# Two-layer attention and FFN kernel: the maximum chunks of the second layer in pairs on the two row halves of the array, and the query product in double parts

## The chip, the cores and the metric

The kernel runs on one core of a Trainium2 chip. The metric is device time in microseconds (us) from one launch to its end; the median of three runs is taken. The profile is one further execution of the same program.

## The reference, cut to what matters

Two layers run over a sequence of 8 batches of 100 tokens of 256 features; each has a cross attention and a feed-forward part. The change lies in the cross attention of the second layer (16 heads, 1444 keys for each batch, 64 latent dimensions):

```python
q_hk  = (hidden_q @ Wq.T).reshape(Bv, Sv, H, K)
q_big = rope(einsum('bshk,hkq->bshq', q_hk, w_kc_q))       # 192 wide
kv_r  = rope(kv_c)                                         # 64 wide
q_r   = einsum('bshq,hqr->bhsr', q_big, W_qr)
k_r   = einsum('bld,hdr->bhlr', kv_r, W_kr)
scores = einsum('bhsr,bhlr->bhsl', q_r, k_r)
attn   = softmax(scores, axis=-1)
ctx_c  = einsum('bhsl,bld->bhsd', attn, kv_r)
...
```

The kernel multiplies the weights of the query side together beforehand, so that a query meets the 64 roped key values directly. The softmax subtracts a maximum for each query, and any value near the largest score serves, since it cancels in the quotient.

## The kernel before

The second layer is worked in 16 **periods** u, two for each batch b; a period holds 8 heads of 100 queries, 800 columns. It has 24 **slots** (`LANE`), numbered `at` = 0 to 23, or s = 0 to 47 through a batch. In each slot k the function `scores(k)` puts one block of 120 keys by 400 queries in bank 0 or 1 of PSUM, as two matmuls (line 1167): a first one of 128 rows, in which the high parts of the queries meet the high and low parts of the keys (called *hi* below), and a second of 65 rows for the low parts of the queries and the maximum (*lo*). ACT takes the exponential of the block (line 1631). `scores(k)` waits until ACT has done block k - 2. After every eighth slot, `values` sums four double blocks into the context on the two column halves of the array (line 1179). POOL adds the weights up, off to the side.

While period u runs, three things are made ready for later ones, each laid into the slots by hand:

- **The maximum of period u + 1.** Seven blocks of 128 queries (the last has 32) times three stretches of 482 keys make 21 chunks (`MC`). A chunk c is one matmul of 128 rows (line 1147, `max_chunk`), into banks 3 and 4 in turn, and one reduction on DVE (line 1931, `reduce_max`). It stands in slot `at` = 1 + c. A chunk waits for the reduction of the chunk two before it. After the last, in slot 21, `join_max` takes the maximum of the three columns (line 1938); in slot 23 `turn_max` on PE waits for it and transposes it (line 1153). ACT copies that out, and a DMA lays it down as the row that the scores of u + 1 use.
- **The query product of period u + 2**, `q_big`, in six parts in the slots `at` = 1 to 6 and 9 to 14 (lines 1091 and 1096, four matmul instructions a part), then `rope` on DVE after slots 7 and 15, and `q_latent` after slot 23 (line 1118).
- **The FFN of batches before**: attention output in slots s = 17 to 20 (line 1202), gate and up product, and on DVE `residual` in slot s = 21 (lines 1956 to 1960), `quantise_x` in s = 23, `quantise_h` in s = 13, 17, 20 and 23.

Every engine works off its own queue in program order and waits on semaphores. An instruction that waits holds back all that stands behind it on its engine. The chunks of period 0 have no slots to lie in: they run in a stretch ahead of the loop, with `q_big` and `rope` of period 1 among them.

## Time and profile before

| | |
|---|---|
| median of three runs | 955.08 us (953.51 to 961.84) |
| profiled execution | 955.46 us, of which the span of the trace is 953.7 |
| PE (TensorE matmul) busy | 847.4 us, 89% of the span |
| DVE (VectorE) busy | 582.8 us, 61% |
| POOL busy | 448.9 us, 47% |
| ACT (ScalarE) busy | 415.9 us, 44% |
| mean granted clock of TensorE | 0.93 |

The loop over the 16 periods runs from 321.7 us to about 926 us. A period takes between 29 and 42 us. Matmuls are pipelined: the time of one in the trace runs from its start to its modelled end, so what a matmul costs the engine is read from the start of one to the start of the next. The line numbers in the tables are those of the kernel before.

### The profile page before, as it was taken

The numbers are of one execution on the slowest core, as the hardware profiler recorded it, in microseconds if no ns is written. First come the engines' busy times: TensorE is split into PE (matmuls) and PEld (weight loads), VectorE is DVE, ScalarE is ACT, GpSimd is POOL, SyncE is SP. The second block draws the span as 40 slices with busy tenths as digits, with TensorE's granted clock in tenths as the row PEclk, the third lists the DMA queues.
The fourth block names the chain that finished last, engine by engine and source line by source line (L and its number), as shares of the span: only waits on it lengthen the run. The fifth ranks groups of instructions, "written<-read, shape, count | busy, mean of one in ns | idle before, by whom it ended". The sixth has DMA issues, their size and how long they took to land.

```text
span 953.7 us, 15582 instructions
## 1 busy us (share of the span) xinstructions
PE 847.4 (89%) x5844; PEld 629.2 (66%) x5844; DVE 582.8 (61%) x1112; ACT 415.9 (44%) x896; POOL 448.9 (47%) x465
## 2 busy tenths in 40 slices
PE   4998879989987799998989889899898988989884
PEld 3666756888965567766767667676676766766442
DVE  3537854222275567577587588668658748757445
ACT  2357851212121354544534544554454463454531
POOL 3000006500050187767657576666675755557530
PEclk8879989989997799999989999999999999999976
DMA  9560026589310000000000000010000000000000
GB/s 194 184 198 2 2 64 241 208 303 344 109 36 17 16 2 11 20 7 10 17 9 10 21 10 2 10 30 1 10 22 10 10 5 10 2 14 10 8 6 9
DMA packets 42167, 52.28 MB, mean 55 GB/s; under 512 B 12230, under 2 KB 35704, under 8 KB 41836
## 3 DMA queue, kind: packets, MB, share of 16 engines
q1 hardware_dynamic: 41068, 49.63, 16.6%
q0 software_dynamic: 1024, 1.64, 0.6%
q8 instruction: 47, 0.77, 0.3%
q14 instruction: 28, 0.23, 0.1%
HBM read 45.80 MB, written 5.36 MB: 54 GB/s over the span
## 4 chain that ended last, share of the span: by engine, by line
PE 68%; DVE 16%; ACT 7%; issue 4%; DMA 3%; POOL 1%; POOLq 0%; SPq 0%; DVEq 0%; ACTq 0%
PE ps L1167 13%; PE ps L1179 10%; PE ps L1147 7%; PE ps L1091 5%; PE ps L1015 5%; PE ps L1202 3%; PE ps L1118 3%; PE ps L969 3%; PE ps L1028 3%; PE ps L1096 2%; DVE nm L1931 2%; ACT sm L1424 2%; DMA xs<-xs_scratch 2%; DVE xyz L1902 1%; DVE h L1992 1%
## 5 line engine op out<-in xcount | busy, mean ns | idle before, releaser
L592 POOL TENSOR_TENSOR acc<-acc,pt 120x800 f32<-120x800 f32 (+1 forms) x157 | 301.6, 1921 | 123.5 <-ACT pt L1631 91.3
L1631 ACT ACTIVATE pt<-ps 120x400 f32<-120x400 f32 (+1 forms) x384 | 189.4, 504 | 237.1 <-PE ps L1167 229.4
L1931 DVE TENSOR_REDUCE nm<-ps 128x1 f32<-128x482 f32 (+1 forms) x336 | 215.7, 655 | 109.0 <-PE ps L1147 105.7
L1167 PE MATMUL ps<-qh,khl 128*120 128x400 f32 (+1 forms) x384 | 167.9, 437 | 24.0 <-ACT pt L1631 23.6
L1147 PE MATMUL ps<-khl,qh 128*128 128x482 f32 (+1 forms) x336 | 136.1, 408 | 10.6 <-DVE nm L1931 9.1
L1179 PE MATMUL ps<-pt,kv 120*64 120x400 f32 (+1 forms) x768 | 145.0, 514 | 0.0
L1167 PE MATMUL ps<-ql,kh 65*120 65x400 f32 (+1 forms) x384 | 137.2, 357 | 0.0
L1167 PEld LDWEIGHTS ps<-qh,khl 128*120 128x120 f32 (+1 forms) x384 | 72.9, 190 | 70.6 <-ACT pt L1631 34.3
L1179 PEld LDWEIGHTS ps<-pt,kv 120*64 120x64 f32 (+1 forms) x768 | 52.8, 140 | 66.6 <-issue 58.3
L614 POOL TENSOR_TENSOR rstd<-veps,mhalf 100x1 f32<-100x1 f32 (+2 forms) x19 | 13.0, 682 | 167.5 <-DVE veps L1765 115.4
L1091 PEld LDWEIGHTS ps<-x3T,wqb 128*128 128x128 f32 x512 | 76.6, 195 | 6.7 <-DVE xyz L1902 1.7
L1091 PE MATMUL ps<-x3T,wqb 128*128 128x100 f32 x512 | 75.0, 274 | 2.7 <-ACT x3T L1388 1.4
L1167 PEld LDWEIGHTS ps<-ql,kh 65*120 65x120 f32 (+1 forms) x384 | 73.6, 192 | 4.4
L1147 PEld LDWEIGHTS ps<-khl,qh 128*128 128x128 f32 (+1 forms) x336 | 61.6, 184 | 22.3 <-DVE nm L1931 18.9
L592 POOL TENSOR_TENSOR acc<-pt,pt 121x800 f32<-121x800 f32 x16 | 30.5, 1907 | 93.3 <-ACT pt L1631 93.3
L1015 PE MATMUL ps<-xsT,egu 128*128 128x128 f32 x448 | 53.5, 278 | 1.0 <-DVE hs L1857 0.6
L1015 PEld LDWEIGHTS ps<-xsT,egu 128*128 128x128 f32 x448 | 52.9, 195 | 1.8 <-ACT xsT L1388 1.3
L1202 PE MATMUL ps<-bmat,ct 128*100 128x256 f32 x128 | 38.3, 428 | 13.8 <-DVE ct L1952 13.1
L1912 DVE TENSOR_TENSOR ql<-ps,qh 64x400 fp32r<-64x400 f32 x32 | 18.2, 570 | 49.8 <-ACT qh L1551 49.6
L667 POOL DMA_INDIRECT xn<-ys_scratch,slot x8 | 8.6, 1078 | 81.9 <-DMA ys_scratch<-ysb 79.9
L1902 DVE TENSOR_TENSOR xyz<-ps,ropeq 64x200 f32<-64x200 f32 x128 | 46.2, 361 | 1.3
L1551 ACT ACTIVATE qh<-ps 64x400 fp32r<-64x400 f32 x64 | 31.9, 498 | 31.9 <-PE ps L1118 31.4
(273 smaller groups left out, 1270.5 us busy)
## 6 DMA issues: line engine op xcount, KB each, us to landing
egu<-_L_ffn_gate_up_proj_dram SPq DMA_DIRECT2D x14, 1024.0 KB, 6.0
edn<-in_L_ffn_down_proj_dram SPq DMA_DIRECT2D x14, 512.0 KB, 6.8
spread<-inv_scratch SPq DMA_DIRECT2D x30, 100.0 KB, 2.7
craw<-in_ctx_dram SPq DMA_DIRECT2D x8, 360.0 KB
wo_n<-in_L_xattn_Wo_dram SPq DMA_DIRECT2D x1, 2048.0 KB, 11.3
wq_n<-in_L_xattn_Wq_dram SPq DMA_DIRECT2D x1, 2048.0 KB, 8.0
xs_scratch<-zero SPq DMA_DIRECT2D x1, 1792.0 KB, 9.8
xs<-xs_scratch SPq DMA_DIRECT2D x14, 128.0 KB, 5.9
```

Of the source, the lines that this page charges most:

```text
L592: nc.gpsimd.tensor_tensor(total[r, :, :], before[r, :, :], pt[j % PT_BUF][r, :, :], ALU.add).then_inc(p_added, 1)
L969: last = mm(ps[:, 2 * (k % 2) + a, 0:HT], sgu[:, c, a, 128 * m:128 * m + 128], xnT[:, c, HT * n:HT * n + HT], start=c == 0, stop=c == DC - 1)
L1015: last = mm(ps[:, 2 * (t % 2) + a, TR * m:TR * m + TR], egu[t % EBUF][:, c, FI * a + 128 * m:FI * a + 128 * m + 128], xsT[t % 2][:, c, :], ...
L1091: mm(ps[:, 6, S * part:S * part + S], wqb[:, c, h, 0:128], x3T[:, c, :], start=c == 0, stop=c == DC - 1)
L1147: mm(ps[0:w, 3 + m % 2, 0:MN], qh[u % 2][:, 128 * i:128 * i + w], khl[b % 2][:, MSTART[n]:MSTART[n] + MN], start=True, stop=True).then_inc ...
L1167: last = mm(ps[0:key_rows(t), k % 2, 0:HT], lhs[:, keys], rhs[:, HT * a:HT * a + HT], start=first, stop=not first)
L1179: last = mm(ps[CD * a:CD * a + CD, 2, 0:HT], kv[b % KV_BUF][r, t, :], pt[j % PT_BUF][r, a, :], start=t == 0, stop=t == KT - 1)
L1202: last = mm(ps[0:S, 6, 0:D], ct[:, S * i:S * i + S], bmat[:, i, :], start=i == 0, stop=i == GH - 1)
L1551: last = nc.scalar.activation(qh[u % 2][p:p + CD, HT * a:HT * a + HT], ps[CD * a:CD * a + CD, 5, 0:HT], ACT.Copy)
L1631: nc.scalar.activation(pt[j % PT_BUF][0:rows, k % 2, :], ps[0:rows, k % 2, 0:HT], ACT.Exp).then_inc(p_ready, 1)
L1902: last = tt(o[CD * j:CD * j + CD, 2, e:HG:2, :], ps[CD * e:CD * e + CD, 7, 0:HT // 2].rearrange("p (i q) -> p i q", i=HG // 2), ropeq[CD * ...
L1931: nc.vector.tensor_reduce(nm3[0:w, i, n:n + 1], ps[0:w, 3 + m % 2, 0:MN], AX.X, ALU.max).then_inc(m_reduced, 1)
```

## The change

`max_chunk` becomes `max_pair`. Eleven pairs (`MP`) take the place of 21 chunks, and stand in every second slot, `at` = 2, 4 to 22 (`MAX_AT`). A matmul of a pair has 64 rows instead of 128. The even chunk takes rows 0 to 63 of the array with the high parts of the keys (`kh1`), the odd chunk rows 64 to 127, where `khl` also holds high parts. So the low parts of the keys no longer enter the maximum. The even chunk writes bank 3, the odd one bank 4; the eleventh pair has one chunk only. A pair waits for the reduction of the pair just before it. DVE reads both banks in one instruction of two stretches of 482.

`q_big` stands in slots 1, 3, 5 and 9, 11, 13, two parts at a time.

```diff
--- before.py
+++ after.py
@@ -74,7 +74,9 @@
 GU = 2 * HT
 MT = -(-GU // 128)
 MC = 3 * MT
-MAX_FROM, TURN_MAX_AT = 1, 23
+MP = -(-MC // 2)
+MAX_AT, TURN_MAX_AT = (2, 4, 6, 8, 10, 12, 14, 16, 18, 20, 22), 23
+QB_AT = (1, 3, 5)
 X3_BANK = (4, 7, 5)
 KEEP_AT, INVERT_AT, DIVIDE_AT = 1, 9, 15
 
@@ -1131,21 +1133,23 @@
                                 ident[0:key_rows(t), 0:key_rows(t)])
                 last.then_inc(k_turned, 1)
 
-            def max_chunk(u, c):
-
-                b, p, m = u // PAIRS, u % PAIRS, MC * u + c
-                if c == 0:
+            def max_pair(u, i):
+
+                b, p = u // PAIRS, u % PAIRS
+                if i == 0:
                     pe.wait_ge(q_hi, u + 1)
                     if p == 0:
                         pe.wait_ge(k_kept, 3 * (b + 1))
                     if u:
                         pe.wait_ge(m_kept, u)
-                if m >= 2:
-                    pe.wait_ge(m_reduced, m - 1)
-                i, n = c // 3, c % 3
-                w = m_rows(i)
-                mm(ps[0:w, 3 + m % 2, 0:MN], qh[u % 2][:, 128 * i:128 * i + w], khl[b % 2][:, MSTART[n]:MSTART[n] + MN],
-                   start=True, stop=True).then_inc(m_done, 1)
+                if MP * u + i:
+                    pe.wait_ge(m_reduced, MP * u + i)
+                for c in range(2 * i, min(2 * i + 2, MC)):
+                    q, n, r = c // 3, c % 3, slice(CD * (c % 2), CD * (c % 2) + CD)
+                    w = m_rows(q)
+                    keys = khl if c % 2 else kh1
+                    mm(ps[0:w, 3 + c % 2, 0:MN], qh[u % 2][r, 128 * q:128 * q + w], keys[b % 2][r, MSTART[n]:MSTART[n] + MN],
+                       start=True, stop=True).then_inc(m_done, 1)
 
             def turn_max(u):
 
@@ -1280,9 +1284,9 @@
                 q_big(1, 0, part)
             pe.wait_ge(tails_set, 2)
             pe.wait_ge(fq_kept, 6)
-            for c in range(MC):
-                max_chunk(0, c)
-                if c == MC // 2:
+            for i in range(MP):
+                max_pair(0, i)
+                if i == MP // 2:
                     for part in range(6):
                         q_big(1, 1, part)
             turn_x3(1)
@@ -1293,10 +1297,11 @@
                     k, u, at = SLOTS * b + s, PAIRS * b + s // LANE, s % LANE
                     f, x = at // PHASE, at % PHASE
                     scores(k)
-                    if u + 1 < NU and MAX_FROM <= at < MAX_FROM + MC:
-                        max_chunk(u + 1, at - MAX_FROM)
-                    if u + 2 < NU and f < 2 and 1 <= x <= 6:
-                        q_big(u + 2, f, x - 1)
+                    if u + 1 < NU and at in MAX_AT:
+                        max_pair(u + 1, MAX_AT.index(at))
+                    if u + 2 < NU and f < 2 and x in QB_AT:
+                        for part in range(2):
+                            q_big(u + 2, f, 2 * QB_AT.index(x) + part)
                     if b + 1 < B and s in KEY_SLOT:
                         turn_keys(b + 1, KEY_SLOT.index(s))
                     if b + 2 < B and s == X_SLOT:
@@ -1921,18 +1926,19 @@
                 tt(khl[b % 2][0:CD, k0:k0 + n], ps[0:CD, 5, 0:n], kh1[b % 2][0:CD, k0:k0 + n].bitcast(F32), ALU.subtract)\
                     .then_inc(k_kept, 1)
 
-            def reduce_max(u, c):
-
-                if c == 0 and u:
+            def reduce_max(u, i):
+
+                if i == 0 and u:
                     dve.wait_ge(max_ready, u)
-                m, i, n = MC * u + c, c // 3, c % 3
-                w = m_rows(i)
-                dve.wait_ge(m_done, m + 1)
-                nc.vector.tensor_reduce(nm3[0:w, i, n:n + 1], ps[0:w, 3 + m % 2, 0:MN], AX.X, ALU.max).then_inc(m_reduced, 1)
+                n = min(2, MC - 2 * i)
+                w = m_rows(2 * i // 3)
+                dve.wait_ge(m_done, MC * u + 2 * i + n)
+                nc.vector.tensor_reduce(nm3[:, :, :].rearrange("p i n -> p (i n)")[0:w, 2 * i:2 * i + n], ps[0:w, 3:3 + n, 0:MN],
+                                        AX.X, ALU.max).then_inc(m_reduced, 1)
 
             def join_max(u):
 
-                dve.wait_ge(m_reduced, MC * (u + 1))
+                dve.wait_ge(m_reduced, MP * (u + 1))
                 if u >= 2:
                     dve.wait_ge(m_turned, u - 1)
                 nc.vector.tensor_reduce(nmx[u % 2][:, :], nm3[:, :, :], AX.X, ALU.max, negate=True).then_inc(max_ready, 1)
@@ -2025,13 +2031,13 @@
             low_keys(0, 2)
             low_q(0)
             dve.wait_ge(tails_set, 2)
-            for c in range(MC):
-                if c == 1:
+            for i in range(MP):
+                if i == 1:
                     rope(1, 0)
-                reduce_max(0, c)
-                if c == MC // 2:
+                reduce_max(0, i)
+                if i == MP // 2:
                     norm_x3(1)
-                if c == MC // 2 + 2:
+                if i == MP // 2 + 1:
                     rope(1, 1)
             join_max(0)
             low_q(1)
@@ -2041,9 +2047,9 @@
                     f, x = at // PHASE, at % PHASE
                     if u and u + 1 < NU and at == 0:
                         low_q(u + 1)
-                    if u + 1 < NU and MAX_FROM <= at < MAX_FROM + MC:
-                        reduce_max(u + 1, at - MAX_FROM)
-                        if at == MAX_FROM + MC - 1:
+                    if u + 1 < NU and at in MAX_AT:
+                        reduce_max(u + 1, MAX_AT.index(at))
+                        if at == MAX_AT[-1]:
                             join_max(u + 1)
                     if b >= 2 and s == HN_SLOT:
                         hidden_norm(b - 2)
```

On PE, at the start of the period u = 3 (slots 0 to 2). Before:

```order
L1167 MATMUL ps<-qh_192,khl_188 121x400
L1167 MATMUL ps<-ql_194,kh_190 121x400
L1167 MATMUL ps<-qh_192,khl_188 121x400
L1167 MATMUL ps<-ql_194,kh_190 121x400
L1147 MATMUL ps<-khl_187,qh_191 128x482
L1091 MATMUL ps<-x3T,wqb 128x100 x2
L1167 MATMUL ps<-qh_192,khl_188 121x400
L1167 MATMUL ps<-ql_194,kh_190 121x400
L1147 MATMUL ps<-khl_187,qh_191 128x482
L1091 MATMUL ps<-x3T,wqb 128x100 x2
```

After:

```order
L1171 MATMUL ps<-qh_192,khl_188 121x400
L1171 MATMUL ps<-ql_194,kh_190 121x400
L1171 MATMUL ps<-qh_192,khl_188 121x400
L1171 MATMUL ps<-ql_194,kh_190 121x400
L1093 MATMUL ps<-x3T,wqb 128x100 x4
L1171 MATMUL ps<-qh_192,khl_188 121x400
L1171 MATMUL ps<-ql_194,kh_190 121x400
L1151 MATMUL ps<-kh_189,qh_191 128x482
L1151 MATMUL ps<-khl_187,qh_191 128x482
```

Slot 1 has lost its chunk and holds two parts of the query product; slot 2 holds both chunks of the first pair, one behind the other.

On PE, the end of the period u = 4, slots 21 to 23 and the transpose of the maximum. Before:

```order
L1167 MATMUL ps<-qh_191,khl_187 120x400
L1167 MATMUL ps<-ql_193,kh_189 120x400
L1147 MATMUL ps<-khl_187,qh_192 32x482
L1167 MATMUL ps<-qh_191,khl_187 120x400
L1167 MATMUL ps<-ql_193,kh_189 120x400
L1167 MATMUL ps<-qh_191,khl_187 120x400
L1167 MATMUL ps<-ql_193,kh_189 120x400
L1153 MATMUL ps<-ident,nmx_207 7x128
```

After:

```order
L1171 MATMUL ps<-qh_191,khl_187 120x400
L1171 MATMUL ps<-ql_193,kh_189 120x400
L1171 MATMUL ps<-qh_191,khl_187 120x400
L1171 MATMUL ps<-ql_193,kh_189 120x400
L1151 MATMUL ps<-kh_189,qh_192 32x482
L1171 MATMUL ps<-qh_191,khl_187 120x400
L1171 MATMUL ps<-ql_193,kh_189 120x400
L1157 MATMUL ps<-ident,nmx_207 7x128
```

The last chunk of the maximum has moved one slot nearer to the transpose that needs its result.

On DVE, the same place, from `quantise_h` of slot 20 on. Before:

```order
L1931 TENSOR_REDUCE nm_205<-ps 32x1 x2
L2000 TENSOR_SCALAR h_214<-h_214,qsc 100x1024
L1931 TENSOR_REDUCE nm_205<-ps 32x1
L1938 TENSOR_REDUCE nmx_207<-nm_205 128x7
L1956 TENSOR_TENSOR x_sb<-x_sb,ps 100x256
L1958 BN_STATS stats_80<-x_sb 100x6
L1959 BN_AGGR mv_81<-stats_80 100x2
L1960 TENSOR_SCALAR veps_82<-mv_81 100x1
L1966 TENSOR_SCALAR xn_210<-x_sb,mv_81 100x256
```

After:

```order
L1936 TENSOR_REDUCE nm_205<-ps 32x2
L2006 TENSOR_SCALAR h_214<-h_214,qsc 100x1024
L1962 TENSOR_TENSOR x_sb<-x_sb,ps 100x256
L1964 BN_STATS stats_80<-x_sb 100x6
L1965 BN_AGGR mv_81<-stats_80 100x2
L1966 TENSOR_SCALAR veps_82<-mv_81 100x1
L1936 TENSOR_REDUCE nm_205<-ps 32x1
L1944 TENSOR_REDUCE nmx_207<-nm_205 128x7
L1972 TENSOR_SCALAR xn_210<-x_sb,mv_81 100x256
```

The four operations of `residual` stood behind the joined maximum and now stand ahead of its last reduction.

## Rows read from the trace of the kernel before

Some names: in the tables a line such as L1147 is a chunk's matmul, L1167 a score matmul (`qh,khl` is *hi*, `ql,kh` is *lo*), L1091 a part of `q_big`, L1179 `values`, L1118 `q_latent`, L1153 `turn_max`.

**Rows 1.** Page, part 4: the chain that ended last, shares by engine.

```profile
PE 68%; DVE 16%; ACT 7%; issue 4%; DMA 3%; POOL 1%; POOLq 0%; SPq 0%; DVEq 0%; ACTq 0%
```

**Rows 2.** Groups by form, DVE, 500 to 700 us: count | busy, mean ns | idle before.

```profile
L1931 DVE TENSOR_REDUCE nm<-ps 128x1 f32<-128x482 f32 x90 | 58.2, 658 | 28.0 <-PE ps L1147 27.3
...
L1994 DVE TENSOR_REDUCE qsc<-h 100x1 f32<-100x1024 f32 x2 | 2.4, 1208 | 0.0
```

**Rows 3.** Timeline of PE, slots with chunks alone: start, us, engine, line, op.

```profile
610.66 0.38 PE L1147 MATMUL ps<-khl,qh 128*128 128x482 f32 x1
610.88 0.34 PE L1167 MATMUL ps<-qh,khl 128*120 128x400 f32 x1
611.06 0.35 PE L1167 MATMUL ps<-ql,kh 65*120 65x400 f32 x1
611.25 0.38 PE L1147 MATMUL ps<-khl,qh 128*32 128x482 f32 x1
614.63 0.66 PE L1167 MATMUL ps<-qh,khl 128*120 128x400 f32 x1 [3.01 <-ACT pt L1631]
```

**Rows 4.** Timeline of PE, one slot with a q_big part.

```profile
600.84 0.42 PE L1167 MATMUL ps<-qh,khl 128*120 128x400 f32 x1
601.10 0.35 PE L1167 MATMUL ps<-ql,kh 65*120 65x400 f32 x1
...
601.88 0.42 PE L1167 MATMUL ps<-qh,khl 128*120 128x400 f32 x1
```

**Rows 5.** Timeline of PE around a block of values (128x64 halves).

```profile
604.61 0.34 PE L1073 MATMUL ps<-ident,xn 100*128 100x100 f32 x2
604.88 2.91 PE L1179 MATMUL ps<-pt,kv 120*64 120x400 f32 x16
607.71 0.45 PE L1167 MATMUL ps<-qh,khl 128*120 128x400 f32 x1
608.00 0.35 PE L1167 MATMUL ps<-ql,kh 65*120 65x400 f32 x1
```

**Rows 6.** Timeline of PE, 32-row groups of the array, layer 1.

```profile
62.51 0.96 PE L773 MATMUL ps<-kT,qT 32*100 32x100 f32 x32 [0.57 <-issue]
```

**Rows 7.** Timeline of PE, last period: slots without chunks.

```profile
912.68 0.44 PE L1167 MATMUL ps<-qh,khl 128*120 128x400 f32 x1
...
913.90 0.44 PE L1167 MATMUL ps<-qh,khl 128*120 128x400 f32 x1 [0.23 <-ACT pt L1631]
```

**Rows 8.** Timeline of PE, end of a period (u = 4).

```profile
496.36 0.38 PE L1147 MATMUL ps<-khl,qh 128*32 128x482 f32 x1
...
499.21 0.28 PE L1153 MATMUL ps<-ident,nmx 128*7 128x128 f32 x1
```

**Rows 9.** Timeline of DVE, the same stretch.

```profile
496.77 0.65 DVE L1931 TENSOR_REDUCE nm<-ps 32x1 f32<-32x482 f32 x1 [0.85 <-PE ps L1147]
497.35 0.73 DVE L2000 TENSOR_SCALAR h<-h,qsc 100x1024 f32<-100x1024 f32 x1
498.30 0.65 DVE L1931 TENSOR_REDUCE nm<-ps 32x1 f32<-32x482 f32 x1 [0.22 <-PE ps L1147]
498.98 0.17 DVE L1938 TENSOR_REDUCE nmx<-nm 128x7 f32<-128x21 f32 x1
499.07 0.41 DVE L1956 TENSOR_TENSOR x_sb<-x_sb,ps 100x256 f32<-100x256 f32 x1
...
500.28 0.35 DVE L1966 TENSOR_SCALAR xn<-x_sb,mv 100x256 f32<-100x256 f32 x1
```

**Rows 10.** Waits of PE, 320 to 900 us: in total, times, longest.

```profile
PE ps L1167 <- ACT pt L1631: 20.2, 10, 3.0
PE ps L1202 <- DVE ct L1952: 13.1, 6, 2.8
```

**Rows 11.** Timeline of DVE, the maxima ahead of the loop.

```profile
293.14 0.66 DVE L1931 TENSOR_REDUCE nm<-ps 128x1 f32<-128x482 f32 x1
...
317.38 0.18 DVE L1938 TENSOR_REDUCE nmx<-nm 128x7 f32<-128x21 f32 x1
```


## The prediction

> **What bounds the kernel now.** I read the page's chain of waits first: 68% of the chain that ended last is PE, 16% DVE [rows 1]. So PE's own time counts nearly everywhere in the loop, and DVE's where PE waits for it. The second view is PE's timeline, from which I take the start of one matmul to the start of the next. In a slot that holds scores and a chunk, *hi* takes 0.18, *lo* 0.19 and the chunk 0.22: 0.59 us [rows 3]. A slot with a part of `q_big` on top takes 1.04, and *hi* to *lo* is there 0.26 instead of 0.18, since *hi* follows another kind of matmul [rows 4]; that leaves 0.38 for the part. Third, the floor under a slot: in the last period two slots of bare scores take 1.22 [rows 7]. PE waits there for ACT, two banks being all that scores have, so emptying slots below 0.61 each gains nothing. Fourth, the waits of PE: 20.2 us on ACT and 13.1 on the divided context [rows 10]; the wait on the maximum's reductions is too short to stand among them. DVE takes 0.658 us for a chunk [rows 2], against slots of 0.59 to 1.04: it keeps up, just.
>
> **The change, part by part.**
>
> *The matmuls of a pair.* Does the array run both halves at once? The trace before has no 64-row pair of this type. Two near cases overlap. `values`, on two column halves, gets through 16 instructions of 400 columns in 2.83 [rows 5], 0.044 for each 100 columns, against 0.38 / 4 = 0.095 for an instruction of `q_big` of the same type with 100 columns on the whole array [rows 3, 4]. In layer 1, 32 instructions on four 32-row groups take 0.96 [rows 6], under 0.03 each. So I take the two streams of a pair as one: 0.22 instead of 0.44.
>
> *The change of mode around a pair.* Scores use the whole array, a pair halves; each pair is one way in and one way back. Price, from the block of `values`: two transposes start at 604.61 and should last 0.18, `values` starts at 604.88, 0.09 late. Its 16 instructions of 400 columns should need, at 0.0417 for 100 columns (two cycles of 2.4 GHz a column, which the 0.095 of `q_big` is near to, and two halves at once), 2.67; scores start after 2.83, 0.16 late; and *hi* to *lo* is 0.29 instead of 0.18, another 0.11 [rows 5]. Together 0.36. I take 0.33 for a pair, which has no second pass to line up. Bounds: 0.15 (a row half that loads while the array drains) and 0.40. A pair is then 0.22 + 0.33 = 0.55 against 0.44, 0.11 more; ten full pairs in a period make +1.1.
>
> The Trainium skill, TensorEngine Tiling (Array Packing), Theoretical Speedup, gives up to 2x for a contraction of 64, which would favour this change; the same page says under Key Properties that changing the mode drains the engine, with no price. By the first alone a pair would save 0.22, by the second with the trace's price it loses 0.11. The rows of `values` show both, the overlap and the drain, so the sum goes with them.
>
> *`q_big` in double parts.* The same instructions, in 6 slots instead of 12. Six fewer returns to *hi*, each 0.26 - 0.18 = 0.08 [rows 3, 4]: -0.5 a period. `rope` still starts after slot 7, its inputs being ready earlier (slot 5); no gain behind it, since the reductions ahead of it on DVE are the same work.
>
> Together +0.6 in each of the 14 periods with `q_big` (u = 0 to 13): 8.4. In six of them PE waits for the divided context in slot 17 [rows 10], which comes from DVE, and hides what PE lost in slots 13 to 16, about 0.25 each: -1.5. **Term A: +7** (-18 to +18 over the bounds).
>
> *DVE's reductions.* One instruction of 964 values instead of two of 482. From 0.658 for 482 and 1.208 for 1024 [rows 2] a value costs 1.01 ns, so 1.15 against 1.32. It saves 1.7 a period of an engine that is 61% busy. Where DVE is late (slots 12 to 17 of even periods) the count of values between is the same, so PE's wait in slot 17 stays. Taken at nothing.
>
> *One pair in flight.* Before, chunk m waited for chunk m - 2. Now a pair waits for the pair just before. The circle is: pair to reduction 0.49 (a chunk's went from 496.36 to 496.77 [rows 8, 9], and the second matmul of a pair starts later by up to 0.08), reduction 1.15, back to PE 0.08 (an estimate, such as lies between the join at 498.98 + 0.17 and `turn_max` at 499.21): 1.72. With `q_big` two slots take about 2.1 and cover it; so does attention output in slots 17 to 20. It shows where slots are thin: two slots of 0.55 + 4 x 0.18 = 1.3. That is u = 14 (five intervals), u = 1 (three) and u = 0 (one or two), each 0.45 longer. **Term B: +4** (1 to 9; the high end if low keys and `quantise_h` on DVE push reductions past the next pair).
>
> *The end of a period, `turn_max`.* This is the large term. `turn_max` on PE stands ahead of `q_latent` and `values`, and waits for the joined maximum. Before, the last chunk lay in slot 21; now it lies in slot 22, and on DVE `residual` of slot 21 has come ahead of it. For u = 4: the chunk of slot 20 started at 496.36 and `turn_max` at 499.21 [rows 8]. With the change, on DVE: reduction of the pair of slot 20 from 496.85 (the chunk's was at 496.77) to 498.00; `quantise_h` until 498.95 (it takes 0.95 to the next start); `residual` 1.21 (499.07 to 500.28), until 500.16; last reduction 0.65, 500.81; join 0.2; `turn_max` at 501.07 [rows 9]. That is 1.86 later. PE itself would be there at about 499.4, so this is a wait of 1.7, and nothing later gives it back: what follows on PE (`q_latent`, `values`, next scores) moves with it. It meets the six periods u = 4, 6 to 14: 11.2. In u = 2, without `quantise_h`, 1.86 - 0.95, about 1. In u = 0 and the seven odd periods there is no `residual`; from the last chunk to `turn_max` 0.49 + 0.65 + 0.2 + 0.06 = 1.4 must pass, and PE fills 0.55 + 0.45 with its work; 0.4 is left, partly there before (0.2 in u = 4), and part of these stretches runs at the low clock, where PE is the slower: 0.3 each, 2.4. **Term C: +15** (7 to 20).
>
> *Ahead of the loop.* The 21 chunks of period 0 run at DVE's pace from 293.14 to 317.38 [rows 11]. 21 reductions of 0.658 are 13.8, two ropes and a norm the rest, with a wait for `q_big`. Now ten times 1.15 and 0.65, 12.2, saves 1.6, but seven or eight pairs with nothing of DVE's between them expose 0.57 each, 4.3. **Term D: +2.6** (0 to 5).
>
> Low keys, `quantise_x` and `turn_xq` keep their places; ACT, POOL and the DMAs have no instruction moved. I take all of that at nothing; it is covered by PE's 2.1 us between pairs, and without that cover a low-key step of 0.6 would come on top once.
>
> **Sum:** 7 + 4 + 15 + 2.6 = 28.6 on the profiled 955.46, which is 0.4 above the median of 955.08: 983.7. Forecast **983 us**, 2.9% slower.
>
> **The rivals.**
>
> *The halves pay (faster).* If the change of mode costs a row pair 0.02 instead of 0.33, a pair is 0.24, saves 0.20, and A is 14 x (-2.0 - 0.5) = -35. With B, C and D: -13, 942. Break-even of the whole is a price of 0.13: A then is 14 x (10 x (0.35 - 0.44) - 0.5) = -20. For it: the layer 1 groups overlap well [rows 6]. Against: 0.36 for a block of `values` [rows 5]. By the page's 2x alone it would come out here. Chance 0.12.
>
> *No wait at `turn_max`.* If DVE is earlier there, or slot 22 and 23 are held by ACT anyway (two bare slots need 1.22 [rows 7]), C falls to 1 or 2: 970. Against: the order of DVE's queue leaves no way around `residual`. Chance 0.14.
>
> *The clock falls.* After a wait of 3.01 the next *hi* took 0.66 instead of 0.42 [rows 3, 4], so the granted clock had gone to the lower level. If the 1.7 us waits of six periods do that too, for as long as the waits on ACT did, some 1.7 more each: +10, 993. Chance 0.17.
>
> *The two 64-row matmuls run one after the other.* A pair is 0.44 + 0.33, 0.33 more, A is 14 x (3.3 - 0.5) = 39: 1016. No row shows this type of matmul on row halves, all others overlap. Chance 0.07.
>
> The forecast itself: 0.50.
>
> **The numbers.** About 1% (9.6 us) is what this kernel's runs can tell from no change. Faster by over 1%: the first rival and a little of A's low end, 0.15. Within 1%: A near its low end with a small C, 0.14. Slower: 0.71. For 8 in 10 I leave out the sequential case and most of the fast one: 955 to 1001, which takes in A at a price of 0.15 (965) and the clock rival with its own spread.
>
> **What the profile after would show.** Right: both matmuls of a pair start within some 0.05 of each other; *lo* to the next *hi* around a pair is near 0.75 to 0.8 in all; PE waits 1.5 to 2 for the joined maximum before `turn_max` in even periods from u = 4; reductions take 1.15; the stretch ahead of the loop ends some 2.5 later. Wrong: a pair costing PE under 0.4; no wait before `turn_max`; the slots 17 to 20 of even periods shorter than before; or a stall that I have not placed, since DVE has one pair of slack less in every slot.

## The result

The changed kernel takes 1021.12 us (median of 4, 1013.51 to 1023.43) against 954.3 for the kernel before: 7.1% slower, ratio 1.0709, 95% interval 1.0654 to 1.0765. The forecast was 983 with a range up to 1001. The direction was right, and less than half of the size. Medians and ratios here leave out runs that lie more than 1.5% above the fastest of their kernel, which meets two of the six runs of e2 and one of the four of e4.

In the kernel after, the lines stand a little lower: L1171 is the score matmuls, L1151 a matmul of a pair, L1093 and L1098 the query product, L1206 attention output, L1120 `q_latent`, L1183 `values`, L1157 `turn_max`; on DVE L1936 is the reduction and L1944 the join. In the runs below the numbers shift again by a few lines.

The page of the profile after, parts 1, 4 and 5 (busy time; chain; count | busy, mean ns | idle before). The span is 1021.5 us, 67.8 more than before.

```profile
PE 895.8 (88%) x5844; PEld 603.8 (59%) x5844; DVE 561.9 (55%) x952; ACT 415.9 (41%) x896; POOL 448.8 (44%) x465
...
PE 69%; DVE 14%; ACT 7%; issue 5%; DMA 4%; POOL 1%; SPq 0%; POOLq 0%; ACTq 0%; DVEq 0%
...
L1936 DVE TENSOR_REDUCE nm<-ps 128x2 f32<-128x964 f32 (+2 forms) x176 | 195.7, 1112 | 190.5 <-PE ps L1151 190.0
...
L1151 PE MATMUL ps<-kh,qh 64*128 64x482 f32 (+1 forms) x176 | 89.0, 506 | 18.3 <-DVE nm L1936 18.3
```

DVE does what was forecast: a reduction of two banks takes 1.112 us on the mean over all forms, 21 us less busy time in all. PE is still 69% of the chain [rows 1]. A matmul of a pair stands at 506 ns, against some 400 for a chunk before.

PE's timeline after, slots 1 to 3 of the period u = 7 (start, us, engine, line):

```profile
618.72 1.03 PE L1093 MATMUL ps<-x3T,wqb 128*128 128x100 f32 x8
619.53 0.42 PE L1171 MATMUL ps<-qh,khl 128*121 128x400 f32 x1
619.79 0.35 PE L1171 MATMUL ps<-ql,kh 65*121 65x400 f32 x1
620.07 0.48 PE L1151 MATMUL ps<-kh,qh 64*128 64x482 f32 x1
620.08 0.48 PE L1151 MATMUL ps<-khl,qh 64*128 64x482 f32 x1
620.49 0.44 PE L1171 MATMUL ps<-qh,khl 128*121 128x400 f32 x1
620.77 0.35 PE L1171 MATMUL ps<-ql,kh 65*121 65x400 f32 x1
620.96 1.03 PE L1093 MATMUL ps<-x3T,wqb 128*128 128x100 f32 x8
```

The two matmuls of a pair start 0.01 us apart: the halves do overlap. But from *lo* to the pair is 0.28, from the pair to the next *hi* 0.42, and *hi* to *lo* 0.28; before it was 0.19, 0.22 and 0.18 [rows 3]. That is 0.62 above a pair of slots without chunks, where two chunks cost 0.44. And the eight instructions of a double query part take 0.81 (620.96 to about 621.77), two single parts 0.76.

The end of the even period u = 6. First PE, then DVE:

```profile
610.46 0.40 PE L1151 MATMUL ps<-kh,qh 64*32 64x482 f32 x1
...
611.07 0.35 PE L1171 MATMUL ps<-ql,kh 65*120 65x400 f32 x1
612.78 0.28 PE L1157 MATMUL ps<-ident,nmx 128*7 128x128 f32 x1 [1.36 <-DVE nmx L1944]
```

```profile
608.83 1.15 DVE L1936 TENSOR_REDUCE nm<-ps 32x2 f32<-32x964 f32 x1 [3.10 <-PE ps L1151]
609.91 0.73 DVE L2006 TENSOR_SCALAR h<-h,qsc 100x1024 f32<-100x1024 f32 x1
610.67 0.42 DVE L1962 TENSOR_TENSOR x_sb<-x_sb,ps 100x256 f32<-100x256 f32 x1
...
611.88 0.64 DVE L1936 TENSOR_REDUCE nm<-ps 32x1 f32<-32x482 f32 x1
612.55 0.17 DVE L1944 TENSOR_REDUCE nmx<-nm 128x7 f32<-128x21 f32 x1
```

This is the order of [rows 8, 9] with `residual` (L1962) ahead of the last reduction (L1936), and it cost about what was worked out: from the reduction of the pair of slot 20 to `turn_max` 612.78 - 608.83 = 3.95, where the prediction had 501.07 - 496.85 = 4.22. PE idles 1.36 in front of it, where the prediction had 1.7. The same wait stands in front of `turn_max` in each of the six periods forecast, the even ones from u = 4 to 14, at 1.34 to 1.36.

The waits of PE from 340 to 960 us (total, times, longest), and the circle of one pair in the thin slots of u = 14 (L1151 on PE):

```profile
PE ps L1157 <- DVE nmx L1944: 9.1, 8, 1.4
PE ps L1151 <- DVE nm L1936: 3.3, 7, 1.1
```

```profile
936.05 0.48 PE L1151 MATMUL ps<-kh,qh 64*128 64x482 f32 x1 [0.37 <-DVE nm L1936]
...
937.82 0.48 PE L1151 MATMUL ps<-kh,qh 64*128 64x482 f32 x1 [0.36 <-DVE nm L1936]
```

1.77 from pair to pair, against 1.72 in the prediction. The whole period u = 14, before and then after (the columns of this view are the stretch, its length, then busy time and count of PE, PEld, DVE, ACT and POOL, the granted clock, DMA share and GB/s):

```profile
858.86:888.32 29.46, 28.46 (x141) 17.64 (x139) 22.46 (x44) 13.83 (x29) 20.42 (x12) 1.00 0.03 8
...
920.82:956.74 35.92, 32.59 (x140) 16.82 (x138) 22.45 (x34) 13.54 (x29) 22.13 (x13) 0.90 0.03 6
```

It grew by 6.5 us, and part of it now lies at the lower clock. Where TensorE runs at the lower clock (granted 0.50 from 300 to 324 us), the circle is longer. Here is DVE ahead of the loop:

```profile
296.11 1.16 DVE L1936 TENSOR_REDUCE nm<-ps 128x2 f32<-128x964 f32 x1 [0.16 <-PE ps L1151]
...
303.89 1.16 DVE L1936 TENSOR_REDUCE nm<-ps 128x2 f32<-128x964 f32 x1 [0.89 <-PE ps L1151]
305.94 1.16 DVE L1936 TENSOR_REDUCE nm<-ps 128x2 f32<-128x964 f32 x1 [0.89 <-PE ps L1151]
...
324.10 0.17 DVE L1944 TENSOR_REDUCE nmx<-nm 128x7 f32<-128x21 f32 x1
```

Between 303.89 and 305.94 it is 2.05. The stretch from first reduction to join takes 28.0, against 24.2 before [rows 11]. It also begins 3.0 later (296.11 against 293.14), with no edit of the change ahead of it: over the traces of all runs here that first reduction starts anywhere from 287.3 to 299.5 us. Two single executions can differ by that much before the second layer begins.

Last, one stretch at the end of an odd period (u = 7): slot 19, where PE waits 3 us for ACT, up to the start of the next period (the same view as for u = 14). Before:

```profile
611.47:623.86 12.39, 9.35 (x78) 6.29 (x77) 4.31 (x8) 7.50 (x14) 7.97 (x8) 0.86 0.12 38
```

After (it begins a little earlier, in slot 18):

```profile
645.60:661.60 16.00, 12.56 (x81) 7.62 (x79) 4.76 (x7) 7.71 (x14) 8.03 (x8) 0.68 0.11 30
```

The mean granted clock is 0.86 before and 0.68 after. With the two levels at 1 and 0.5 (2.4 and 1.2 GHz), that is 12.39 x 0.14 x 2 = 3.5 us at the lower one before, and 16.0 x 0.32 x 2 = 10.2 after. The same 3 us wait is followed by three times as long a low stretch. Over the fifteen periods u = 0 to 14 the mean granted clock is 0.97 before (321.68 to 888.32) and 0.92 after (328.13 to 956.74), some 34 and 99 us at the lower level. Of the 65 more, 37 lie in the odd periods and 20 in u = 0 and u = 14, the periods with thin slots, which had none before.

### The profile page after: what moved, and what is told of

Its sections match the earlier page's. It is cut to its first block, busy times and chain, and to the rows that moved or that the text cites. A ratio compares the mean times of both kernels' runs of the same rounds, so it can differ in the third digit from the quotient of the medians.

```text
span 1021.5 us, 15422 instructions
## 1 busy us (share of the span) xinstructions
PE 895.8 (88%) x5844; PEld 603.8 (59%) x5844; DVE 561.9 (55%) x952; ACT 415.9 (41%) x896; POOL 448.8 (44%) x465
## 4 chain that ended last, share of the span: by engine, by line
PE 69%; DVE 14%; ACT 7%; issue 5%; DMA 4%; POOL 1%; SPq 0%; POOLq 0%; ACTq 0%; DVEq 0%
PE ps L1171 14%; PE ps L1183 11%; PE ps L1151 7%; PE ps L1093 6%; PE ps L1120 5%; DVE nm L1936 4%; PE ps L1017 3%; PE ps L1206 3%; PE ps L1098 2%; PE ps L971 2%; DMA xs<-xs_scratch 2%; ACT sm L1429 2%; PE ps L1030 2%; DVE xyz L1907 1%; DVE h L1998 1%
## 5 line engine op out<-in xcount | busy, mean ns | idle before, releaser
L1936 DVE TENSOR_REDUCE nm<-ps 128x2 f32<-128x964 f32 (+2 forms) x176 | 195.7, 1112 | 190.5 <-PE ps L1151 190.0
L1171 PE MATMUL ps<-qh,khl 128*120 128x400 f32 (+1 forms) x384 | 179.3, 467 | 25.4 <-ACT pt L1636 25.0
L1183 PE MATMUL ps<-pt,kv 120*64 120x400 f32 (+1 forms) x768 | 146.1, 517 | 0.0
L1171 PE MATMUL ps<-ql,kh 65*120 65x400 f32 (+1 forms) x384 | 141.3, 368 | 0.0
L1171 PEld LDWEIGHTS ps<-qh,khl 128*120 128x120 f32 (+1 forms) x384 | 74.5, 194 | 95.2 <-issue 55.8
L1151 PE MATMUL ps<-kh,qh 64*128 64x482 f32 (+1 forms) x176 | 89.0, 506 | 18.3 <-DVE nm L1936 18.3
L1183 PEld LDWEIGHTS ps<-pt,kv 120*64 120x64 f32 (+1 forms) x768 | 53.3, 141 | 67.0 <-issue 64.5
L1151 PE MATMUL ps<-khl,qh 64*128 64x482 f32 (+1 forms) x160 | 80.9, 506 | 0.0
L1171 PEld LDWEIGHTS ps<-ql,kh 65*120 65x120 f32 (+1 forms) x384 | 76.4, 199 | 2.7
L1151 PEld LDWEIGHTS ps<-kh,qh 64*128 64x128 f32 (+1 forms) x176 | 31.3, 178 | 71.8 <-issue 44.5
L1093 PE MATMUL ps<-x3T,wqb 128*128 128x100 f32 x512 | 67.9, 278 | 2.7 <-ACT x3T L1393 1.4
L1093 PEld LDWEIGHTS ps<-x3T,wqb 128*128 128x128 f32 x512 | 67.8, 196 | 3.7 <-ACT x3T L1393 1.6
L1206 PE MATMUL ps<-bmat,ct 128*100 128x256 f32 x128 | 41.7, 457 | 14.5 <-DVE ct L1958 13.9
L1120 PE MATMUL ps<-xyz,amat 128*64 128x100 f32 x768 | 49.1, 301 | 4.3 <-DVE h L1988 2.2
```

Of the source, the lines that this page charges most:

```text
L1093: mm(ps[:, 6, S * part:S * part + S], wqb[:, c, h, 0:128], x3T[:, c, :], start=c == 0, stop=c == DC - 1)
L1120: last = mm(ps[CD * a:CD * a + CD, 5, S * i:S * i + S], amat[:, 2 * HG * p + HG * a + i, j, :], xyz[a][:, j, i, :], start=j == 0, stop=j == 2)
L1151: mm(ps[0:w, 3 + c % 2, 0:MN], qh[u % 2][r, 128 * q:128 * q + w], keys[b % 2][r, MSTART[n]:MSTART[n] + MN], start=True, stop=True).then_in ...
L1171: last = mm(ps[0:key_rows(t), k % 2, 0:HT], lhs[:, keys], rhs[:, HT * a:HT * a + HT], start=first, stop=not first)
L1183: last = mm(ps[CD * a:CD * a + CD, 2, 0:HT], kv[b % KV_BUF][r, t, :], pt[j % PT_BUF][r, a, :], start=t == 0, stop=t == KT - 1)
L1206: last = mm(ps[0:S, 6, 0:D], ct[:, S * i:S * i + S], bmat[:, i, :], start=i == 0, stop=i == GH - 1)
```

## The experiments

Each was timed beside runs of the kernel before on the same chip; ratios are to those. The expectations name three theories. Theory 1 is the matmuls' own cost, above all the change of mode for the halves; theory 2 is the late slots and the single pair in flight; theory 3 is the low clock.

**e3: double query parts alone**, in the kernel before.

```diff
-                    if u + 2 < NU and f < 2 and 1 <= x <= 6:
-                        q_big(u + 2, f, x - 1)
+                    if u + 2 < NU and f < 2 and x in (1, 3, 5):
+                        for part in range(2):
+                            q_big(u + 2, f, x - 1 + part)
```

> The kernel before with the double query parts alone (slots 1, 3, 5 and 9, 11, 13), chunks as before. My prediction had this as a gain of 0.5 a period, 7 us: 947. The trace of the changed kernel shows eight instructions of a double part 0.11 apart, four of a single part 0.09 apart: if a part alone hides its weight loads behind the long matmuls around it, this costs 0.15 to 0.2 x 84: 12 to 17 us more than before, 967 to 971.

951.08 against 951.08, ratio 0.9963 (0.9919 to 1.0006): nothing. Neither the gain of my prediction nor the loss expected here. PE's timeline of two slots:

```profile
599.64 0.35 PE L1167 MATMUL ps<-ql,kh 65*120 65x400 f32 x1
599.82 0.38 PE L1147 MATMUL ps<-khl,qh 128*128 128x482 f32 x1
600.04 1.03 PE L1096 MATMUL ps<-x3T,wqt 128*128 128x100 f32 x8
600.85 0.43 PE L1167 MATMUL ps<-qh,khl 128*120 128x400 f32 x1
```

The double part takes 0.81, two single ones 2 x 0.38; what the single parts save in themselves, their slots lose again with *hi* to *lo* at 0.26. Two slots are 2.07 here and 2.06 before [rows 4].

**e4: halves alone.** Every chunk of the kernel before on one half of the rows (high key parts alone), old slots, one at a time.

```diff
-                mm(ps[0:w, 3 + m % 2, 0:MN], qh[u % 2][:, ...], khl[b % 2][:, ...],
+                r = slice(CD * (m % 2), CD * (m % 2) + CD)
+                keys = khl if m % 2 else kh1
+                mm(ps[0:w, 3 + m % 2, 0:MN], qh[u % 2][r, ...], keys[b % 2][r, ...],
```

> The kernel before with each chunk on one half of the rows (even chunks rows 0 to 63, odd chunks rows 64 to 127, high key parts), all in the old slots, one at a time. No overlap can happen, each of 21 chunks pays a way in and a way out. At 0.33 to 0.4 each (theory 1), 315 chunks in the loop cost 105 to 125 us, less what slots hide, about 90: 1045. If the mode costs little (under 0.1), 955 to 985. The low clock would show whether half rows hold it down: stretches longer than 3.4 us behind the waits on ACT.

1047.83 us, ratio 1.0949 (1.0835 to 1.1063), by the ratio 91 us more. PE's timeline:

```profile
644.38 0.35 PE L1169 MATMUL ps<-ql,kh 65*120 65x400 f32 x1
644.66 0.48 PE L1149 MATMUL ps<-khl,qh 64*128 64x482 f32 x1
645.06 0.44 PE L1169 MATMUL ps<-qh,khl 128*120 128x400 f32 x1
645.34 0.34 PE L1169 MATMUL ps<-ql,kh 65*120 65x400 f32 x1
645.61 0.48 PE L1149 MATMUL ps<-kh,qh 64*128 64x482 f32 x1
```

One 64-row chunk between full-array matmuls makes 0.28 + 0.40 + 0.28 (*lo* to chunk, chunk to *hi*, *hi* to *lo*), against 0.19 + 0.22 + 0.18 before. The way in and out costs 0.37. For 315 chunks that is 117, of which slots hid some. And a pair occupies 0.42 where this one chunk occupies 0.40: the second half is nearly free, the first is dear. The Trainium skill, TensorEngine Tiling (Array Packing), Key Properties, says that changing the mode drains the engine; these rows fit that, and give the price. What in the change takes the time (draining, loading weights or both) no run here separates.

**e1: pairs on the full array.** The changed kernel, 128 rows for both matmuls of a pair, one behind the other.

```diff
-                    keys = khl if c % 2 else kh1
-                    mm(ps[0:w, 3 + c % 2, 0:MN], qh[u % 2][r, ...], keys[b % 2][r, ...],
+                    mm(ps[0:w, 3 + c % 2, 0:MN], qh[u % 2][:, ...], khl[b % 2][:, ...],
```

> The changed kernel, with one thing undone: both matmuls of a pair use all 128 rows (high and low key parts, as before the change), so nothing overlaps and the array never changes its mode for them. Slots, one pair in flight and double query parts stay. If the change of mode costs more than the overlap saves (theory 1: a pair costs PE about 0.63 with its way in and out, against 0.44 in sequence), this is faster than the changed kernel by about 0.15 to 0.2 x 160 = 25 to 30 us: near 992. If half rows also hold the granted clock down, the low stretches after the 3 us waits on ACT shrink too and it comes to 975 to 985. If the late slots and the single pair in flight are all that costs (theory 2), it stays at 1015 to 1035.

1000.86 us, ratio 1.0477 (1.039 to 1.0564). 20 to 22 us come back, less than the 25 to 30 that theory 1 expected; 46 stay. Neither theory is enough alone.

**e2: odd slots.**

```diff
-MAX_AT, TURN_MAX_AT = (2, 4, 6, 8, 10, 12, 14, 16, 18, 20, 22), 23
-QB_AT = (1, 3, 5)
+MAX_AT, TURN_MAX_AT = (1, 3, 5, 7, 9, 11, 13, 15, 17, 19, 21), 23
+QB_AT = (2, 4, 6)
```

> The changed kernel with its pairs in slots 1, 3 to 21 instead of 2, 4 to 22, and the double query parts in slots 2, 4, 6 and 10, 12, 14. The last pair then stands in slot 21, ahead of the residual on DVE. Theory 2 (the wait at the transpose of the maximum, 9.1 us in eight waits, and the low clock that follows from thin slots at the end) expects 10 to 20 us less than the changed kernel, 1001 to 1011. If the matmuls' own cost is the whole (theory 1), 1015 to 1025.

982.89 us, ratio 1.0289 (1.0186 to 1.0392): some 38 us come back, and 40 by the ratio, far more than the 10 to 20 expected. PE's wait at `turn_max` falls from 9.1 to 0.8 us. The six runs lie from 980 to 1002, the widest spread of all kernels here, so this figure is the least certain one.

**e5: the residual behind the join.** `RESIDUAL_SLOT` 21 becomes 22, which puts it behind the last reduction and the join on DVE. Nothing else.

```diff
-OUT_FROM, RESIDUAL_SLOT, QX_SLOT, X4_SLOT = 17, 21, 23, 19
+OUT_FROM, RESIDUAL_SLOT, QX_SLOT, X4_SLOT = 17, 22, 23, 19
```

> The changed kernel with the residual on DVE moved by one slot, behind the joined maximum; pairs and everything else as changed. My term for the residual at the end of even periods was 1.2 of a wait of 1.7 in six or seven periods: about 8 us. The trace of the changed kernel has 9.1 us of wait there in eight periods. If that term stands: 1010 to 1014. If the wait is filled by something else: 1018 to 1024.

1016.79 us, ratio 1.0646 (1.0579 to 1.0713). The wait at `turn_max` falls from 9.1 to 3.6 us in total, and the time by about 4 (6 by the ratio), with intervals that overlap. That lies between the two expectations.

**e6: e1 and e2 together.**

```diff
-MAX_AT, TURN_MAX_AT = (2, 4, 6, 8, 10, 12, 14, 16, 18, 20, 22), 23
-QB_AT = (1, 3, 5)
+MAX_AT, TURN_MAX_AT = (1, 3, 5, 7, 9, 11, 13, 15, 17, 19, 21), 23
+QB_AT = (2, 4, 6)
...
-                    mm(ps[0:w, 3 + c % 2, 0:MN], qh[u % 2][r, ...], keys[b % 2][r, ...],
+                    mm(ps[0:w, 3 + c % 2, 0:MN], qh[u % 2][:, ...], khl[b % 2][:, ...],
```

> Both undone together: pairs on all 128 rows and in slots 1, 3 to 21 (query parts in 2, 4, 6). What is left of the change is one reduction for two banks, hence one pair in flight, and double query parts, which alone cost nothing. If the costs add (halves 20, late slots 32 of 67 us): 968 to 972, and the 15 to 20 us above the kernel before are the price of one pair in flight, ahead of the loop and in thin slots. If the halves and the late slots shared one cause (low clock), it stays at 980 to 990.

978.52 us, ratio 1.0253 (1.0201 to 1.0305). From e1 to e6 is 22 us, from e2 to e6 only 4, with e2 as uncertain as said: the parts do not simply add, and 23 us stay. The circle of one pair in its thin slots (u = 14, PE):

```profile
882.41 0.71 PE L1150 MATMUL ps<-khl,qh 128*128 128x482 f32 x2 [0.52 <-DVE nm L1935]
...
884.38 0.71 PE L1150 MATMUL ps<-khl,qh 128*128 128x482 f32 x2 [0.26 <-DVE nm L1935]
```

Nearly 2 us from pair to pair, since here the two matmuls run one behind the other within the circle.

**e10: two in flight.** e6 with one reduction for each chunk, and chunk m waiting for the reduction of m - 2.

```diff
-                if MP * u + i:
-                    pe.wait_ge(m_reduced, MP * u + i)
                 for c in range(2 * i, min(2 * i + 2, MC)):
+                    if MC * u + c and (c > 1 or u):
+                        pe.wait_ge(m_reduced, max(MC * u + c - 1, 1) if c != 0 else MC * u)
...
-                nc.vector.tensor_reduce(nm3[...][0:w, 2 * i:2 * i + n], ps[0:w, 3:3 + n, 0:MN], AX.X, ALU.max)
+                for j in range(n):
+                    dve.wait_ge(m_done, MC * u + 2 * i + j + 1)
+                    nc.vector.tensor_reduce(nm3[...][0:w, 2 * i + j:2 * i + j + 1], ps[0:w, 3 + j, 0:MN], AX.X, ALU.max)
```

> The kernel of e6 (pairs on all rows, odd slots) with one reduction for each chunk and the wait of the kernel before (chunk m for the reduction of m - 2). All that is left of the change is that chunks stand two to a slot, and query parts too. One pair in flight was my explanation of what e6 keeps above the kernel before, 23 us. If it is right: 954 to 960. If it is the bunching in pairs itself that costs, 970 to 978.

966.7 us, ratio 1.0116 (1.0072 to 1.016), between the two expectations. 12 us belong to one pair in flight, ahead of the loop as well as in it: by the traces of e6 and e10 the stretch from first reduction to join falls from 28.6 to 23.2, u = 1 from 32.8 to 31.7 and u = 14 from 32.2 to 29.8. 11 us more belong to chunks standing two to a slot.

**e8: the kernel before with fillers.** Matmuls whose results nobody reads, in front of the two 3 us waits.

```diff
+            def fill(bank, n):
+                for _ in range(n):
+                    mm(ps[:, bank, 0:112], ident_bf[:, :], ident_bf[:, 0:112], start=True, stop=True)
...
+                    if 1 <= b < B - 1 and s == 43:
+                        pe.wait_ge(m_reduced, MC * (u + 1) + 17)
+                        fill(3 + MC * (u + 1) % 2, 48)
                     scores(k)
...
+                    if b in (2, 3, 5, 6) and s == OUT_FROM:
+                        pe.wait_ge(k_kept, 3 * (b + 2))
+                        fill(5, 48)
```

> The kernel before, plus matmuls whose results nobody reads: 48 of 112 columns (bf16, about 2.5 us) in front of the scores of slot 43 of batches 1 to 6, and 48 in front of the attention output in batches 2, 3, 5 and 6, where PE otherwise waits about 3 us for ACT or DVE and its granted clock then drops for 3.4 us or more. The output is the reference's. If the wait is what brings the clock down, ten low stretches of 3.4 us go, each worth up to 1.7: 940 to 945 against 954. If the clock follows something else, or the fillers delay the next instruction: 954 to 960.

941.07 us, ratio 0.9848 (0.9806 to 0.989): 1.5% faster than the kernel before. PE in slots 18 and 19 of u = 7, and a stretch to the next period that begins one slot ahead of the one above:

```profile
604.60 0.38 PE L1147 MATMUL ps<-khl,qh 128*128 128x482 f32 x1
604.82 2.53 PE L1153 MATMUL ps<-ident_bf 128*128 128x112 bf16 x48
607.17 0.42 PE L1172 MATMUL ps<-qh,khl 128*120 128x400 f32 x1
```

```profile
604.00:616.60 12.60, 11.60 (x133) 8.53 (x131) 5.29 (x9) 8.89 (x15) 8.98 (x8) 1.00 0.14 39
```

The 48 fillers lie from 604.82 to 607.17. Of the wait for ACT, one slot later, 0.58 us is left. The two *hi* behind the fillers take 0.42 and 0.45, where the one behind the wait took 0.66 [rows 3], and the clock is granted in full. From the chunk of slot 18 to the next period it is 12.0 us, against 13.2 before (610.66 [rows 3] to 623.86).

**e9: the changed kernel with fillers** (36 in slot 43, bank 3, and 48 in slot 17).

```diff
+                    if 1 <= b < B - 1 and s == 43:
+                        pe.wait_ge(m_reduced, MP * (u + 1) + 9)
+                        fill(3, 36)
                     scores(k)
...
+                    if b in (2, 3, 5, 6) and s == OUT_FROM:
+                        pe.wait_ge(k_kept, 3 * (b + 2))
+                        fill(5, 48)
```

> The changed kernel with the same fillers (36 in slot 43, since both maximum banks are in use at first, and 48 in slot 17). In it the low stretches behind these waits last 6.8 to 10.2 us. If the low clock is a large part of the 67 us (theory 3), it gains more than the kernel before does: 25 to 35 us, 986 to 996. If not, it gains as much as that one, 10 us or less: 1010 or more.

997.65 us, ratio 1.0458 (1.0406 to 1.0511). It gains 23 us, the kernel before 14.5. So 9 us of the 67 are the longer low stretches behind these two waits, by whole times. The fillers do not hold the clock everywhere: in u = 1 to 13 it is at 1.00 in both kernels, but the changed one keeps its 13.7 us of lower clock in u = 0 (none in e8), and has 13.7 in u = 14, which is 40.1 long here and was 35.9 without fillers. The periods u = 6 and 7 in full, first e9, then e8:

```profile
561.11:603.04 41.93, 39.88 (x297) 26.50 (x295) 32.95 (x54) 18.88 (x39) 26.35 (x24) 1.00 0.02 6
603.04:643.26 40.22, 38.05 (x284) 24.92 (x282) 21.95 (x34) 19.99 (x37) 26.10 (x25) 1.00 0.07 19
...
539.27:578.16 38.89, 38.39 (x296) 29.26 (x295) 32.55 (x62) 18.85 (x39) 24.48 (x21) 1.00 0.03 7
578.16:616.61 38.45, 37.06 (x296) 28.14 (x294) 24.75 (x45) 19.64 (x37) 28.00 (x28) 1.00 0.07 19
```

At a full clock they are 3.0 and 1.8 us longer than in e8. Of that, slot 23, with `turn_max`, has 1.35 and 0.71.

**e7: q_latent ahead of turn_max** in the changed kernel, PE's order in slot 23 alone.

```diff
-                    if u + 1 < NU and at == TURN_MAX_AT:
-                        turn_max(u + 1)
                     if x == PHASE - 1:
                         if f == 2 and u + 2 < NU:
                             q_latent(u + 2)
+                        if u + 1 < NU and at == TURN_MAX_AT:
+                            turn_max(u + 1)
```

> The changed kernel with q_latent of slot 23 put ahead of the transpose of the maximum on PE, so that the wait for the joined maximum lies behind 2.1 us of work. The trace has 9.1 us of wait there in eight periods, and with the fillers slot 23 was 1.35 longer in even and 0.7 longer in odd periods than in the kernel before, 14 in all. If nothing later is short of the row of maxima, 14 us less: 1007; with less low clock behind it down to 1000. If the row, which a DMA lays down, now comes too late for the first scores of the next period, the gain is lost: 1015 to 1025.

1022.14 us, ratio 1.0701 (1.0655 to 1.0746): nothing gained. Yet the wait had gone from all periods but u = 14, which has no `q_latent`; PE's waits, and the odd end of u = 7:

```profile
PE ps L1157 <- DVE nmx L1944: 1.4, 1, 1.4
```

```profile
646.80:663.50 16.70, 12.88 (x80) 7.73 (x78) 5.03 (x8) 7.73 (x14) 8.05 (x8) 0.69 0.01 3
```

**e13: the same edit with the fillers.**

```diff
-                    if u + 1 < NU and at == TURN_MAX_AT:
-                        turn_max(u + 1)
...
                             q_latent(u + 2)
+                        if u + 1 < NU and at == TURN_MAX_AT:
+                            turn_max(u + 1)
...
+                    if 1 <= b < B - 1 and s == 43:
+                        pe.wait_ge(m_reduced, MP * (u + 1) + 9)
+                        fill(3, 36)
                     scores(k)
...
+                    if b in (2, 3, 5, 6) and s == OUT_FROM:
+                        pe.wait_ge(k_kept, 3 * (b + 2))
+                        fill(5, 48)
```

> The changed kernel with the fillers (slots 43 and 17) and with q_latent ahead of the transpose. Without fillers, putting q_latent first gained nothing (1022), though the wait for the maximum went from 9.1 us to 1.4. If the low clock ate that gain (its stretches in odd periods grew from about 10 to 13 us), it shows now that the clock is held up: 10 to 14 us under the filled kernel's 998, 984 to 988. If the wait only moves to the row of maxima or to another engine, it stays at 995 to 1000.

984.02 us, ratio 1.0324 (1.0278 to 1.037): 13.6 under e9. First a stretch like that of e7, beginning one slot earlier; then the periods u = 6 and 7 in full:

```profile
624.00:637.80 13.80, 11.38 (x120) 7.19 (x119) 5.13 (x8) 8.69 (x14) 8.90 (x8) 1.00 0.01 3
...
556.47:597.14 40.67, 39.98 (x294) 26.51 (x294) 31.50 (x48) 18.79 (x39) 25.11 (x22) 1.00 0.07 17
597.14:637.76 40.62, 38.18 (x284) 24.75 (x283) 23.20 (x37) 19.91 (x37) 27.35 (x27) 1.00 0.03 7
```

Clock 0.69 without fillers and 1.00 with them. But most of the 13.6 us is not what the edit gains at a held clock. Set beside e9, u = 6 is 1.2 shorter and u = 7 is 0.4 longer; over u = 1 to 13, where the clock is full in both, the edit gains 3.0 us. Of the 11.1 us between the two spans, 4.4 lie ahead of the loop and 3.5 in u = 14, which the edit does not touch and which has 6.8 us of lower clock here against 13.7 in e9. The gain is small because the wait moves: PE's waits for the maximum at `turn_max` fall from 11.5 to 1.4 us (340 to 960 us), and those of `q_latent` for DVE grow from 2.8 to 6.8. In e7 the even periods u = 6, 8 and 10 gain 1.1 to 1.2 as well, and the odd ones from u = 5 on lose 0.7 to 1.9; its lower clock there and in u = 0 and 14 is as long or longer than in the changed kernel.

**e12: fillers ahead of the loop too** (8 behind each chunk of period 0 from the third on), in the kernel of e8.

```diff
                 max_chunk(0, c)
+                if c >= 2:
+                    fill(0, 8)
```

> The kernel before with the fillers of slots 43 and 17, and 8 more fillers behind each chunk of the stretch ahead of the loop from the third on, where DVE sets the pace, PE waits and its granted clock is at the lower level for 20 of 30 us. Query product and q_latent in that stretch take 4.9 and 3.8 us there where 2.2 and 2.3 are their times at the higher level. If the clock stays up: 4 us less than with the first fillers, 937. If the fillers get in the way of chunks: 941 to 946.

940.07 us, ratio 0.9843 (0.9805 to 0.9881), no different from e8. From first reduction to join it is 23.1 us, against 24.1 in e8.

**e14: e10 with fillers** (slot 43, and slot 17 of batches 2 to 6).

```diff
+                    if 1 <= b < B - 1 and s == 43:
+                        pe.wait_ge(m_reduced, MC * (u + 1) + 17)
+                        fill(3, 48)
                     scores(k)
...
+                    if b in (2, 3, 4, 5, 6) and s == OUT_FROM:
+                        pe.wait_ge(k_kept, 3 * (b + 2))
+                        fill(5, 48)
```

> The kernel of e10 (chunks two to a slot on all rows, odd slots, two in flight) with fillers in slots 43 (48) and 17 (48, batches 2 to 6). It was 11 us above the kernel before; its trace has the same matmul times in the query slots, but an extra wait of 3 us in slot 17 of one period and longer low stretches behind slot 17. If bunching costs only through the clock, it comes near the filled kernel before: 942 to 947. If it costs by itself: 950 to 955.

950.5 us, ratio 0.9949 (0.992 to 0.9979), where bunching was expected to come out if it costs by itself: 9.4 over e8, 16 under e10. So most of what bunching costs stays with the fillers. By the traces of e14 and e8 it is 0.6 us or less in most periods, but 2.6 in u = 0 (6.8 us of lower clock, none in e8), 2.2 in u = 8 and 1.8 in u = 14, both of these mainly in slot 17.

## Why the prediction was wrong

What the bound is, PE's own time with DVE close behind, held. So did the overlap of the halves, and the sign.

Where the 67.8 us between the two traces lie, in single executions: 6.4 ahead of the loop, 3.0 of them the late start that no edit made; 7.5 in u = 0 and 6.5 in u = 14; 48 in u = 1 to 13; from u = 15 on it is 0.7 shorter. Of the 48, 31 are there at a full clock too (e9 against e8), about 20 in slots 0 to 22 and 11.7 in slot 23; the other 17 go with the lower clock.

One row of single edits leads from the changed kernel to the one before, in ratios to the latter: 1.0709; halves off (e1) 1.0477; odd slots (e6) 1.0253; two in flight (e10) 1.0116; one chunk a slot (e3, double parts kept) 0.9963. That is about 22, 21, 13 and 15 us. Another order shares them out otherwise: by way of e2 (1.0289) the odd slots come first with 40 and the halves have 3, with e2's wide interval. So this row alone does not give the halves their 22; the spacing of the matmuls and the full-clock periods do.

- **Term A, the matmuls and their mode: forecast +7, measured about +20** (slots 0 to 22 of u = 1 to 13 at a full clock, e9 against e8, with about 1 us of term B in u = 1; 22 from the changed kernel to e1). The failed step is "0.22 + 0.33 = 0.55 against 0.44, 0.11 more". A pair costs 0.62, so 0.18 more: in the terms of that sum 0.22 + 0.40, where a single chunk pays 0.37 (e4). I had 0.36 from `values` [rows 5] and rounded it down with no row for it. The mechanism was right, the price was too low. The other half of the failure is "*hi* to *lo* 0.26 - 0.18, six fewer, -0.5 a period": e3 shows no gain, since the double part itself is 0.05 longer and leaves one such interval behind it. 160 pairs x 0.17 to 0.18 are 27 to 29, of which some 20 are seen.
- **Term B, one pair in flight: forecast +4.** The circle was right (1.72, measured 1.77). From e6 to e10 it is worth 12 to 13, but that edit also undoes term D, so the forecast beside it is 6.6; and by the traces u = 1 and u = 14 return 3.5, near the forecast, and the stretch ahead of the loop 5.4. What was too low is the changed kernel itself, where these periods also lie at the lower clock: u = 14 grew from 29.5 to 35.9, 1.3 of it in slot 23, and u = 0 from 35.1 to 42.7, 2.7 of it in slot 23, where PE had been at the full clock.
- **Term C, `turn_max`: forecast +15, measured 13** (slot 23 of u = 1 to 14, e9 against e8; 1.35 in an even period, 0.7 in an odd one). This term held, mechanism and size. But undoing only part of it (e5) or hiding it (e7) returned 4 and 0, and at a full clock hiding it returned 3 (u = 1 to 13 of e13 against e9), since `q_latent` then waits for DVE. The whole shift to late slots is worth 21 to 40, by the order of the edits.
- **Term D, ahead of the loop: forecast +2.6, measured +3.8** to the join (28.0 against 24.2). The rows of after have the circle there at 2.05, nearly all of it at the lower clock.
- **Left out: chunks two to a slot.** I took grouping of the same matmuls as free. With all else undone it is still 11 us over the kernel before (e10) and 9.4 with the fillers (e14 over e8). The cause is not settled. In e10's trace PE waits 2.6 us for the divided context in slot 17 of u = 8, where it waited 1.1 before, with 6.8 us of lower clock behind it, and u = 8 is 4.8 longer; in the plain slots at a full clock the bunched kernel is no slower (u = 2). What makes DVE late there was not tried.
- **The rival "the clock falls": right in kind, wrong in place.** I gave it 1.7 us in six even periods and left it out of the sum. More than half of the extra low time lies in odd periods, behind the wait for ACT that was there before: 3.5 us became 10.2. e9 against e8 puts what the filled stretches cost the change at 9 us, and the periods u = 1 to 13 of the four traces at 17; e13 against e7 shows 38 us between the same program with and without fillers.

The rivals "the halves pay" and "one after the other" fell by the first rows of after; that the second one's sum, 1016, lies near the measured time is chance. Nothing speaks against taking DVE's saved time at nothing.

## What to carry to other kernels

Overlap of half arrays has to pay for the way in and the way out: here 0.37 us for each visit, against 0.20 that the second half saves, so one matmul a half is too few for a visit. The last member of a chain that someone waits for wants slack behind it, and double buffering lost to a wider instruction is a wait in every thin slot. Where a wait on another engine is followed by a low granted clock, harmless matmuls in it can be worth more than the reordering one had in mind (14.5 us in e8, 3 for e13's edit at a full clock). And a difference of two whole times is best split by period, with the granted clock beside it, before it is put down to an edit: of the 11.1 us between the spans of e9 and e13, 3 lay where the edit acts at a full clock.
